# From first attention to first experts in a two-layer Flamingo kernel: order of residual and selection, one-hots by choice, expert numbers last, unread products

## Time and profile before

| what | value |
|---|---|
| median of 3 runs | 1229.87 us (1229.16 to 1230.22) |
| the profiled execution | 1233.03 us, with a span of 1231.3 us from the first to the last instruction |
| TensorE busy | 1169.8 us, 95% of the span |
| VectorE, ScalarE, GpSimd busy | 595.4, 479.4, 391.7 us |
| mean granted clock of TensorE | 0.981 |
| first weights of the experts, each layer | 32 loads of 1028 KB, 52 of 514 KB |

### The profile page before, as it was taken

How to read it: one execution, slowest core, us unless ns; L and a number is a source line. 1 busy time by engine, 2 the same in 40 slices (tenths; PEclk the granted TensorE clock), 3 DMA queues, 4 the chain that set the end, 5 groups by cost and what they waited for, 6 DMA issues and landing times. The chain is left out here.

```text
span 1231.3 us, 29193 instructions
## 1 busy us (share of the span) xinstructions
PE 1169.8 (95%) x11425; PEld 901.6 (73%) x11425; DVE 595.4 (48%) x1437; ACT 479.4 (39%) x1130; POOL 391.7 (32%) x411
## 2 busy tenths in 40 slices
PE   6999999977999999998799999999998999999998
PEld 4767777756999999974466666666665579999975
DVE  5777777774210001057566666567656612111226
ACT  3545555523323332324445444444454232233221
POOL 3666666632223222131101011010011245555420
PEclk9999999977999999999899999999999999999999
DMA  6011111305999998640021000000000459999965
GB/s 182 24 28 36 28 37 44 122 15 190 383 325 337 316 341 315 250 135 19 2 87 30 16 21 21 26 9 9 2 9 14 165 196 349 350 360 353 341 224 168
DMA packets 64392, 180.93 MB, mean 147 GB/s; under 512 B 10176, under 2 KB 36608, under 8 KB 55808
## 3 DMA queue, kind: packets, MB, share of 16 engines
q1 hardware_dynamic: 55088, 156.40, 36.9%
q0 software_dynamic: 8064, 22.03, 5.0%
q10 hardware_dynamic: 1104, 0.64, 0.2%
HBM read 163.11 MB, written 15.93 MB: 145 GB/s over the span
## 5 line engine op out<-in xcount | busy, mean ns | idle before, releaser
L2301 ACT ACTIVATE ex_hT<-kept_psum,ex_w 128x128 f32<-128x128 f32 x464 | 132.9, 369 | 294.8 <-PE kept_psum L2356 157.4
L2356 PE MATMUL kept_psum<-ex_xT,ex_w 128*128 128x128 f32 x1856 | 222.5, 276 | 0.0
L2356 PEld LDWEIGHTS kept_psum<-ex_xT,ex_w 128*128 128x128 f32 x1856 | 215.7, 193 | 0.1
L2367 PE MATMUL kept_psum<-ex_w,ex_hT 128*128 128x256 f32 x928 | 214.0, 379 | 0.0
L2263 DVE TENSOR_TENSOR ex_yt<-kept_psum,ex_b 128x256 f32<-128x256 f32 x84 | 35.7, 425 | 353.6 <-PE kept_psum L2367 353.6
L2367 PEld LDWEIGHTS kept_psum<-ex_w,ex_hT 128*128 128x128 f32 x928 | 170.1, 190 | 19.8
L2229 POOL DMA_INDIRECT ex_results<-ex_yt,ex_to_row x84 | 83.0, 988 | 254.9 <-DVE ex_yt L2263 254.9
L1249 ACT ACTIVATE at_probs<-kept_psum 120x800 f32<-120x800 f32 (+2 forms) x128 | 101.3, 842 | 85.5 <-PE kept_psum L1418 85.5
L1088 DVE TENSOR_REDUCE at_negmax<-kept_psum 100x2 f32<-100x722 f32 x128 | 115.5, 902 | 0.0
L568 ACT ACTIVATE at_probs<-kept_psum 120x800 f32<-120x800 f32 (+1 forms) x96 | 80.1, 837 | 73.7 <-PE kept_psum L691 73.6
L410 DVE TENSOR_REDUCE at_negmax<-kept_psum 120x8 bf16<-120x800 f32 (+1 forms) x96 | 90.6, 985 | 23.4 <-PE kept_psum L682 23.0
(11 more groups left out here) (252 smaller groups left out, 1691.1 us busy)
## 6 DMA issues: line engine op xcount, KB each, us to landing
ex_w<-in_pack_in SPq DMA_DIRECT2D x32, 1028.0 KB
ex_w<-in_pack_out SPq DMA_DIRECT2D x32, 1024.0 KB
ex_w<-in_pack_in SPq DMA_DIRECT2D x52, 514.0 KB
ex_w<-in_pack_out SPq DMA_DIRECT2D x52, 512.0 KB
at_ctx<-in_ctxT SPq DMA_DIRECT2D x31, 361.0 KB, 3.6
ex_normed<-ex_xhat SPq DMA_DIRECT2D x16, 200.0 KB
ex_w<-ex_results SPq DMA_DIRECT2D x6, 400.0 KB
ex_sw<-in_L_ffn_sW SPq DMA_DIRECT2D x2, 1024.0 KB
```

What stands on the lines that cost most here:

```text
L2301: last = act.activation(hT[t % N][:, c, :], ps_h[:, (t * U + u) % N, i * P:(i + 1) * P], ACT.Gelu, bias=w1[t % N][:, B1 + c:B1 + c + 1])
L2356: last = pe.matmul(ps_h[:, (t * U + u) % N, i * P:(i + 1) * P], w1[t % N][:, c * ff + f:c * ff + f + P], xT[t % N][:, c, :], start=(c == 0 ...
L2367: last = pe.matmul(ps_y[:, t % N, 0:D], hT[t % N][:, c, :], w2[t % N][:, c * D:(c + 1) * D], start=(c == 0), stop=(c == FC - 1))
```

## The change

- In round 16 of attention the residual of batch 14 stands ahead of the selection; the selection of the first part is cut in two: its first choice in round 16, its second choice and the mask in round 17, behind the moments of the last pair. Ranks (`lanes`) go from round 17 to round 18.
- On TensorE, in round 17, the turning and routing of the pair 12, 13 stands ahead of `rank_up`.
- Instead of 24 instructions that write one-hot times token number for the first part, VectorE writes all one-hots of one choice in one product (`hot_lanes`, 100x1536), the first choice in round 18, the second behind the selection of the second part; GpSimd multiplies each by the token numbers (`number_lanes`, 100x1536, over the same columns). The second part keeps `in_lanes`.
- The experts' numbers (`experts_of`) are computed behind `in_lanes` of the second part rather than inside `starts`, with one expert less in the comparison. The second layer computes them where it did.
- Unread products: four ahead of the first shift and four ahead of the third in the last batch, fifteen behind `tabulate` of the first layer.

```diff
@@ -489,9 +489,10 @@
         for t in range(B + 4):
             if t == B:
                 prep.normed(dve, PAIRED - 2)
-                prep.route.select(dve, 0)
             if on(t - 2):
                 residual(t - 2)
+            if t == B:
+                prep.route.select(dve, 0, range(1))
             if on(t):
                 maxima(t, 0)
             if t == 0:
@@ -527,9 +528,10 @@
                 dve.wait_ge(x_ready, 2 * p + 2)
                 prep.moments(dve, p)
             if t == B + 1:
+                prep.route.select(dve, 0, range(1, 2))
+            if t == B + 2:
                 prep.route.lanes(dve, 0)
-            if t == B + 2:
-                prep.route.in_lanes(dve, 0)
+                prep.route.hot_lanes(dve, 0, 0)
             if on(t):
                 sums(t, 1)
             if t == LAST:
@@ -623,6 +625,10 @@
                 pe.wait_ge(taken[before], at + 1)
             return ring_bank(name, b)
 
+        def keep_warm(bank, n):
+            for _ in range(n):
+                pe.matmul(bank[:, 0:P], ident[:, :], wk[:, 0, 0:P], start=True, stop=True)
+
         def transposes(b):
             bank = into("xT", b)
             pe.wait_ge(xhat_ready, b + 1)
@@ -746,6 +752,8 @@
             if on(t + 1):
                 transposes(t + 1)
                 project_k(t + 1, 0)
+            if t == LAST:
+                keep_warm(into("sum", LAST - 1), 4)
             if on(t):
                 shift(t, 0, 0)
             if on(t + 1):
@@ -785,10 +795,10 @@
                 project_o(LAST - 1)
                 last_values(range(NJ - 1, NJ))
                 project_o(LAST)
+            if t > B:
+                late_tensor(pe, prep, psum, t)
             if t == B + 1:
                 prep.route.rank_up(pe, 0)
-            if t > B:
-                late_tensor(pe, prep, psum, t)
 
         for name, at in ring[-2:]:
             pe.wait_ge(taken[name], at + 1)
@@ -1839,14 +1852,15 @@
         expert_f = m.sb("expert_f", [1, TILES])
         expert_of = m.sb("expert_of", [1, NT], I32)
         route_step, exp_in, exp_out = m.sem("route_step"), m.sem("exp_in"), m.sem("exp_out")
-        mask_ready, ranks_ready, lanes_ready, tiles_ready, table_ready = (
-            m.sem(n) for n in ("mask_ready", "ranks_ready", "lanes_ready", "tiles_ready", "table_ready"))
+        mask_ready, ranks_ready, tiles_ready, table_ready = (m.sem(n) for n in ("mask_ready", "ranks_ready", "tiles_ready", "table_ready"))
+        lanes_ready = [m.sem(f"lanes_ready{i}") for i in range(len(SPLIT))]
+        hot_ready = m.sem("hot_ready")
         expert_ready, from_ready, rows_ready = (m.sem(n) for n in ("expert_ready", "from_ready", "rows_ready"))
         then = Chain(None, route_step)
         ranks = psum[0:T, rank_bank, 0:(B + 1) * E]
         table = psum[:, 3, 0:top * TILES]
 
-        def select(dve, i):
+        def select(dve, i, ks=range(top)):
             b0, b1 = SPLIT[i]
             bs, n = slice(b0, b1), b1 - b0
             then.eng = dve
@@ -1869,7 +1883,7 @@
                 then(dve.tensor_reduce(norm_sum[:, bs], score, AX, ALU.add))
                 then(dve.reciprocal(norm_rec[:, bs], norm_sum[:, bs]))
                 then(dve.tensor_tensor(score, score, per_expert(norm_rec[:, bs]), ALU.mult))
-            for k in range(top):
+            for k in ks:
                 then(dve.tensor_reduce(value[:, k, bs], score, AX, ALU.max))
                 then(dve.tensor_tensor(logit, score, per_expert(value[:, k, bs]), ALU.is_equal))
                 then(dve.tensor_tensor(logit, logit, per_batch(rev[0:T, :]), ALU.mult))
@@ -1877,6 +1891,8 @@
                 then(dve.tensor_tensor(pick[:, k, bs, :], logit, per_expert(rowmax[:, bs]), ALU.is_equal))
                 if k < top - 1:
                     then(dve.scalar_tensor_tensor(out=score, in0=pick[:, k, bs, :], scalar=BIG, in1=score, op0=ALU.mult, op1=ALU.add))
+            if ks[-1] < top - 1:
+                return
             then(dve.tensor_tensor(chosen, pick[:, 0, bs, :], pick[:, 1, bs, :], ALU.add))
             for k in range(2, top):
                 then(dve.tensor_tensor(chosen, chosen, pick[:, k, bs, :], ALU.add))
@@ -1912,7 +1928,25 @@
                 for b in range(*SPLIT[i]):
                     last = dve.tensor_scalar(in_lane[:, k * B + b, :], minus_lanes[0:T, :], lane_of[:, k, b:b + 1], tok[:, b:b + 1],
                                              ALU.is_equal, ALU.mult)
-                last.then_inc(lanes_ready, 1)
+                last.then_inc(lanes_ready[i], 1)
+
+        def hot_lanes(dve, i, k):
+            b0, b1 = SPLIT[i]
+            dve.tensor_tensor(in_lane[:, k * B + b0:k * B + b1, :], minus_lanes[0:T, :].unsqueeze(1).to_broadcast([T, b1 - b0, P]),
+                              lane_of[:, k, b0:b1].unsqueeze(2).to_broadcast([T, b1 - b0, P]), ALU.is_equal).then_inc(hot_ready, 1)
+
+        def number_lanes(pool, i, k):
+            b0, b1 = SPLIT[i]
+            pool.wait_ge(hot_ready, k + 1)
+            columns = in_lane[:, k * B + b0:k * B + b1, :]
+            pool.tensor_tensor(columns, columns, tok[:, b0:b1].unsqueeze(2).to_broadcast([T, b1 - b0, P]), ALU.mult).then_inc(lanes_ready[i], 1)
+
+        def experts_of(dve):
+            last = E - 1
+            then(dve.tensor_tensor(passed[:, :, 0:last], cols[0:1, 0:TILES].unsqueeze(2).to_broadcast([1, TILES, last]),
+                                   end[0:1, 0:last].unsqueeze(1).to_broadcast([1, TILES, last]), ALU.is_ge))
+            then(dve.tensor_reduce(expert_f[:, :], passed[:, :, 0:last], AX, ALU.add))
+            dve.tensor_scalar(expert_of[:, 0:NT], expert_f[:, :], float(last), None, ALU.min).then_inc(expert_ready, 1)
 
         def starts(dve):
             then.eng = dve
@@ -1922,10 +1956,8 @@
                                           in1=before[0:T, :, :], op0=ALU.subtract, op1=ALU.mult))
             then(dve.tensor_reduce(start[:, :], below[:, :, :], AX, ALU.add))
             then(dve.scalar_tensor_tensor(out=end[:, :], in0=whole_of[:, :], scalar=ROUND, in1=start[:, :], op0=ALU.subtract, op1=ALU.add))
-            then(dve.tensor_tensor(passed[:, :, :], cols[0:1, 0:TILES].unsqueeze(2).to_broadcast([1, TILES, E]),
-                                   end[0:1, :].unsqueeze(1).to_broadcast([1, TILES, E]), ALU.is_ge))
-            then(dve.tensor_reduce(expert_f[:, :], passed[:, :, :], AX, ALU.add))
-            dve.tensor_scalar(expert_of[:, 0:NT], expert_f[:, :], float(E - 1), None, ALU.min).then_inc(expert_ready, 1)
+            if shared:
+                experts_of(dve)
 
         def in_tiles(dve):
             by_choice = picked[:, :, :, :].rearrange("p k b e -> p (k b) e")
@@ -1942,7 +1974,7 @@
             pe.wait_ge(tiles_ready, 1)
             for i, (b0, b1) in enumerate(SPLIT):
                 for k in range(top):
-                    pe.wait_ge(lanes_ready, i * top + k + 1)
+                    pe.wait_ge(lanes_ready[i], k + 1)
                     for b in range(b0, b1):
                         c = k * B + b
                         if k:
@@ -2238,6 +2270,9 @@
                 pool.wait_ge(base_step, B)
                 for n in range(GB):
                     add_shared(n)
+            if not shared:
+                for k in range(top):
+                    route.number_lanes(pool, 0, k)
             for i in range(XR):
                 pool.wait_ge(xhat_saved[i], 16 * len(range(i, PAIRED, XR)))
             pool.wait_ge(from_ready, 1)
@@ -2269,10 +2304,13 @@
                 route.weigh(dve, gates)
             else:
                 route.spread(dve)
+                route.hot_lanes(dve, 0, 1)
             route.starts(dve)
             route.lanes(dve, last)
             route.in_tiles(dve)
             route.in_lanes(dve, last)
+            if not shared:
+                route.experts_of(dve)
             route.rows(dve, from_row, to_row, row_f, empty, later)
             if not shared:
                 route.weigh(dve, gates)
@@ -2411,6 +2449,8 @@
             route.tabulate(pe)
             if early is not None:
                 early.tensor_done(pe)
+                for _ in range(15):
+                    pe.matmul(ps_t[:, 1, 0:P], ident[:, :], early.wa[:, 0, 0:P], start=True, stop=True)
             if shared:
                 shared_long(1)
                 shared_hidden(pe, 2, range(FS - 2, FS - 1))
```

5 lines of the change are left out of this document (4 added, 1 removed).

## The result

Six runs of the changed kernel gave a median of 1238.06 us (1237.05 to 1239.32), six of the kernel before on the same chip 1230.95. The ratio is 1.0058 [1.0045, 1.0070]: slower by more than the 0.2% that can be told, and 3.7 us above the upper end of the range. The profiled execution took 1238.02 us with a span of 1236.3 (before 1233.03 and 1231.3), so the two traces differ by 5.0 us where the medians differ by 7.1. The mean granted clock is 0.986 against 0.981: the changed kernel is slower at a slightly higher clock.

What follows compares the result with a forecast made beforehand. TensorE, busy 95% of the span, was taken as the bound, with the hand-over a serial piece before it. Row numbers -0.15, gather +1.0 and first block +0.75 gave +1.6 on 1229.87: 1231.5 us, range 1227.4 to 1234.4.

Steps and rivals of the forecast that it cites:

- rival 1: Second GpSimd product already catches L1921 in starts: hold 2.85 rather than 1.65, more weights slow; 1233.3 us, chance 0.22.
- the last logits at 274.8: End of the hand-over's routing logits, before at 277.97: 276.2 from the new order, 274.8 with the clock held.
- the contention of the gather: First gather issued beside two fresh weight loads: +1.0 us to its turn, between 0 and 2.4.
- GpSimd's products: Multiplying 1536 one-hot elements by token numbers on GpSimd: 3.0 us each, possibly 2.7 to 3.5.
- The first hold: First number_lanes catches VectorE's is_equal L1877 in the second part's selection, which waits for its end: +2.75 us.
- Where the second hold catches: Second number_lanes, beside starts and lanes of part 2, catches VectorE at the latest at L1906: +1.65 us.
- -1.45 of the eight products: Last attention batch: unread products hold TensorE's clock, everything from 263 on 1.45 us earlier; bounds +0.8 and -2.2.
- -2.28 + 0.54 of the order: Residual before select starts project_o of batch 15 2.28 us earlier; six select steps replacing lanes cost 0.54.
- Rival 3: Clock falls in the last batch all the same, the 1.45 us is not won: 1232.9 us, chance 0.10.
- The expert numbers' steps: Between starts and row numbers: experts_of leaves (0.98), returns before rows as 1.0, covering 0.39 of waiting for tabulate.
- The fifteen products and the first block, +0.75: Products fit TensorE's 4.86 us idle, but a later low clock slows the first weights: +0.75, bounds -1.54 and +2.2.
- rival 2: VectorE is not held beside GpSimd's products; row numbers gain 3.15 us in all: 1228.3 us, chance 0.15.

Runs made afterwards that it cites:

- the one with the loads behind the gather: Changed kernel with the second load of first weights held until the first gather has landed: 1238.70 us, ratio 1.0050.
- the kernel with both undone: Changed kernel without GpSimd's products and with expert numbers computed inside starts again; order and unread products kept: 1230.38 us, ratio 0.9994.
- the one without the fifteen: Changed kernel without GpSimd's products, with early expert numbers, and without the fifteen unread products behind tabulate: 1233.80 us, ratio 1.0017.

## Why the prediction was wrong

It said 1231.5, no change, and rival 1 at 1233.3 was the highest case it had. Two steps failed. The first is the last logits at 274.8, the gain of 3.2 us that was to pay for the rest: 277.81 in the profiled execution. The second is the contention of the gather, put at +1.0: +2.85. These two make 4.9 of the 5.0 us between forecast and measured start of the first weights' matmuls (+0.85 and +5.80). Step by step:

- *GpSimd's products.* Priced at 3.0 us by the earlier trace rows, measured 2.75: right. That VectorE would be held: right for both. The first hold is 2.37 us beyond the step's 0.19 (forecast 2.75). hot_lanes 1.75 (forecast 1.8), lanes and hot_lanes done before the logits: right.
- *Where the second hold catches.* The forecast let it begin at L1906, now L1922, a step with one SBUF input, and took +1.65. It began at L1955 in starts, and held 2.57: **rival 1's mechanism**, whose condition was GpSimd's product within 0.2 us of starts: it came 0.16 behind starts and 0.03 ahead of L1955. From L391, 100x4 elements held by its two SBUF inputs, a scalar_tensor_tensor with two should have been expected to be held too; "no row of this form" was given too much weight. The rule of the Trainium skill that the prediction cited ("SBUF — State Buffer", section "Who interferes with whom") was right here, and the trace agrees: 2.80 us against 0.23 without the product. One pair of rows does not fit it: GpSimd's 100x2 step of 0.70 us at 271.27 has two inputs in SBUF, and two VectorE steps with two SBUF inputs (L1888 at 271.38, L1889 at 271.68) ran beside it in 0.26 us each, as far as so short a GpSimd row can be trusted.
- *Together*, from T0 to the row numbers, +3.15 in the profiled executions. The forecast had 7.6 and 8.6 against 5.94 and 7.33, +2.9. This stretch was forecast well; what should have paid for it was not there.
- *The last logits at 274.8.* This is the term that failed most: they came at 277.81. Its two shares were -1.45 of the eight products and -2.28 + 0.54 of the order. The order's held: 1.6 of 1.74. The products' was worked out as if the low stretch had one cause, the hole, and would be gone with it. In the three traces where the clock stayed high it was (29.1 us from first scores to T0, 2.8 less than before, where 3.2 had been forecast). In the three others, the changed kernel's among them, the low clock came ten us later, onto values and project_o of the same batch: L724 at 2.90 instead of 1.59, L733 at 1.57 instead of 1.11. Rival 3, that the clock falls all the same, had 0.10; in this execution it came true in a stronger form, and took away not only the 1.45 but nearly all of the order's gain. How many of the changed kernel's own six runs went this way is not known, as one of them has a trace.
- *The order.* project_o of batch 15 did start as its input was there, as forecast, and VectorE's steps went as written. The 1.6 us are in the traces, but the kernel with this order alone measures 1.0013 [0.9998, 1.0028]: a gain of that size is not seen in the time. That stretches ahead of the last batch and behind the first weights swallow it is seen in the one trace, and not shown for the median.
- *Contention of the gather, +1.0 between 0 and 2.4.* Measured +2.85 from gather to matmuls (1.96 to the first turn, 0.89 as the second turn waits for its own gather), above the upper bound. The prediction counted only the first gather; the matmuls of the first block need both turns, and the second gather is issued 1.5 us behind the first, into the same loads. Alone on the kernel before, the late numbers cost 3.1 us; with no products, 3.7. This is the second step that failed, a cost that was mis-sized. How loads delay a gather is left open (see the start of its packets above).
- *The expert numbers' steps.* Moved behind the one-hots they cost 1.0 and cover the 0.39: right (6.87 and 6.79 against 7.33).
- *The fifteen products and the first block, +0.75.* They end at 298.81, 5.21 us for the 15 (3.5 and 7.0 were the forecast's two ends) as the clock is low from 293.6 to 297.0, and delay no turn (the turn waits 2.17 for the gather). With the loads early again they matter: in three of four such traces the turn comes right behind them, and 4.71 us behind the gather in one of these, where 3.1 to 3.9 is usual. The +0.75 for the first block is not borne out, as from the matmuls to the end it is 932.6 against 933.4, but that stretch varies by more than this from trace to trace.
- *The lower end of the range.* By its own words (rival 2, less 0.3, less the gather's 1.0) it is 1227.0 and not 1227.4. Nothing hangs on it.

**Added up** in medians: without the GpSimd products the change gains 4.0 us (1238.06 to 1234.10), without the late numbers on top 3.7 (to 1230.38), and these 7.7 are the difference to no change. Both costs are seen from both sides, by undoing and by doing alone (+3.1 to 5.5 for the products, +2.6 to 3.1 for the late numbers), and the stretches in the traces agree. Not settled: why undoing the late numbers alone left the median at 1238.0. Its segment fell by 2.3 us in the one execution whose trace there is, and that execution is one of the two at 1233.3 and 1233.6. These two have a mean granted clock of 0.988 and 0.987, the five others 0.983 to 0.985, so more of their time was at the low clock; where in the program, no trace shows.

## What to carry to other kernels

Before work is handed to GpSimd, look whether VectorE has, meanwhile, a step with two SBUF operands in its critical chain: here 1.0 us of work taken off cost 2.4 to 2.6 us of waiting, twice, and a step on 100x32 elements was held as long as a big one. A transfer that nobody waits for may still make the next one late: before moving a trigger later "because it isn't late", look at what it will then be issued together with, and count every gather that the first block needs. And a low stretch of TensorE's clock that is gone from its place can come back behind it: read the granted clock of the next twenty us as well, in more than one execution, and count stretches from an event near by, not from the start of the program. Here eight products won 1.2 us in three traces and lost 1.4 in three.

## What the runs showed that I had not expected

The same instructions, at different times. The changed kernel, the one with expert numbers early and the one with the loads behind the gather are identical up to T0, and their profiled executions have T0 at 277.81, 274.90 and 275.43. In the first the low clock ran from 259.4 to 266.3 and again from 273.1 on; in the other two the first low stretch after 250 us begins at 269.9 and 270.5. An execution meets such a stretch in the last batch or does not. T0 moves by 3 us between them. Two more sources are told under the table of the last batch: the stretch near 32 us, which four of fourteen executions have, and the time behind the first weights' matmuls. I take these, from these traces and without a trace of every run, for the main part of the spread within one kernel too: the runs of the kernel with both undone go from 1228.38 to 1234.61, those of the one without the fifteen from 1229.22 to 1238.75. A single trace of such a kernel is a sample; what can be compared are stretches between two events near each other (T0 to starts: 7.03 to 7.13 in all six kernels with GpSimd's products, 5.94 to 6.12 in seven of the eight without; first scores to T0 within 0.2 in each group).

The clock also doesn't tell the time by itself: the changed kernel has 0.986 against 0.981 before and is 5 us longer. TensorE is busy for 1173.5 us against 1169.8, unread products among it, and idle for 1.3 us more.
